# GpSimd's work on weight pieces in two halves, small VectorE operations one column at a time

## The reference

```python
q = (x @ Wq) ; k = (x @ Wk) ; v = (x @ Wv)          # 32 heads, 8 kv heads repeated 4 times
probs = softmax(where(causal, q k^T * 128**-0.5, -inf))
x = layernorm(x + (probs @ v) @ Wo)
weights = sparsemax(x @ W_router^T + b_router)       # 8 experts
ffn = x @ W_base^T + b_base + sum_e weights_e * (x @ lora_A_e) @ lora_B_e
out = layernorm(x + ffn)
```

## Time and profile before

| | |
|---|---|
| median of three runs | 689.89 us |
| the profiled execution | 687.37 us |
| its span | 685.3 us |
| TensorE busy with matmuls | 662.2 us (97%) |
| VectorE busy | 543.8 us (79%), 1525 instructions |
| ScalarE busy | 412.8 us (60%) |
| GpSimd busy | 279.7 us (41%), 424 instructions |
| granted TensorE clock, mean | 0.998 |

### The profile page before, as it was taken

How to read it: one execution, slowest core, us unless ns; L and a number is a source line. 1 busy time by engine, 2 the same in 40 slices (tenths; PEclk the granted TensorE clock), 3 DMA queues, 4 the chain that set the end, 5 groups by cost and what they waited for, 6 DMA issues and landing times.

```text
span 685.3 us, 11442 instructions
## 1 busy us (share of the span) xinstructions
PE 662.2 (97%) x3606; PEld 354.1 (52%) x3606; DVE 543.8 (79%) x1525; ACT 412.8 (60%) x1072; POOL 279.7 (41%) x424
## 2 busy tenths in 40 slices
PE   6798999999999999999999999999999999999996
PEld 3364545455554555454555555454555545445675
DVE  4899889876897679767888779767878776899774
ACT  1677566667647765667556764667656764766232
POOL 1576972167105661258004751248014550161132
PEclk9999999999999999999999999999999999999999
DMA  9347347363924256343924366444724335544411
GB/s 291 118 133 167 62 104 181 60 95 61 231 55 93 48 133 159 74 78 87 224 49 77 62 157 121 78 78 95 183 47 77 61 64 108 115 101 75 80 47 61
DMA packets 200780, 71.81 MB, mean 105 GB/s; under 512 B 169744, under 2 KB 192784, under 8 KB 200720
## 3 DMA queue, kind: packets, MB, share of 16 engines
q1 hardware_dynamic: 199376, 70.04, 46.7%
q10 hardware_dynamic: 1344, 1.05, 0.6%
HBM read 27.02 MB, written 2.10 MB: 42 GB/s over the span
## 4 chain that ended last, share of the span: by engine, by line
PE 83%; DVE 7%; DMA 3%; POOL 3%; issue 2%; SPq 1%; ACT 1%; POOLq 0%; DVEq 0%; ACTq 0%
PE bank L1128 21%; PE bank L1079 19%; PE bank L1118 13%; PE bank L1103 11%; PE bank L1091 4%; PE bank L1059 3%; PE bank L1160 3%; DMA pT<-p 2%; PE bank L1072 2%; DVE pr L929 2%; PE bank L1062 2%; DVE p L947 1%; POOL raw L678 1%; SPq L627 1%; PE bank L1171 1%
## 5 line engine op out<-in xcount | busy, mean ns | idle before, releaser
L678 POOL TENSOR_SCALAR raw<-raw,scale_of 128x512 f32<-128x512 f32 x76 | 121.0, 1593 | 162.0 <-ACT wk L740 66.2
L781 ACT ACTIVATE pr<-pr,mx 128x96 f32<-128x96 f32 (+15 forms) x256 | 131.4, 514 | 85.9 <-DVE mx L929 85.9
L790 ACT ACTIVATE p<-pr,ri 128x32 f16<-128x32 f32 (+15 forms) x256 | 118.8, 512 | 78.3 <-DVE ri L939 56.7
L1079 PE MATMUL bank<-xT,wq 128*128 128x512 f16 x720 | 164.4, 379 | 0.2 <-DVE v L849 0.2
L947 DVE SCALAR_TENSOR_TENSOR p<-pr,ri,p 128x256 f16<-128x256 f32 (+15 forms) x256 | 135.2, 572 | 35.2 <-ACT p L790 34.8
L929 DVE CUSTOM_DVE_ANT_0 pr<-bank,mask,back_of 128x32 f32<-128x32 f32 (+15 forms) x256 | 124.6, 494 | 43.3 <-PE bank L1103 42.8
L1103 PE MATMUL bank<-kT,qT 128*128 128x32 f16 (+15 forms) x768 | 124.4, 279 | 5.0 <-DVE qT L843 3.7
L1118 PE MATMUL bank<-pT,v 128*128 128x512 f16 x480 | 123.3, 379 | 3.0 <-DMA pT<-p 2.9
L1079 PEld LDWEIGHTS bank<-xT,wq 128*128 128x128 f16 x720 | 70.3, 98 | 82.2 <-DVE v L849 0.6
L691 POOL MEMSET p<- 128x64 f16 (+2 forms) x192 | 34.3, 206 | 161.8 <-DMA pT<-p 161.8
L1103 PEld LDWEIGHTS bank<-kT,qT 128*128 128x128 f16 x768 | 67.1, 98 | 64.2 <-issue 5.3
(11 more groups left out here) (121 smaller groups left out, 738.8 us busy)
## 6 DMA issues: line engine op xcount, KB each, us to landing
raw<-in_wo SPq DMA_DIRECT2D x32, 256.0 KB, 3.7
raw<-in_wq SPq DMA_DIRECT2D x30, 256.0 KB, 3.9
raw<-in_wk SPq DMA_DIRECT2D x8, 256.0 KB, 3.1
raw<-in_wv SPq DMA_DIRECT2D x8, 256.0 KB, 5.2
y<-in_x SPq DMA_DIRECT2D x1, 2048.0 KB, 13.2
pT<-p SPq DMA_TRANSPOSE x128, 3.7
out<-y SPq DMA_DIRECT2D x8, 256.0 KB, 2.0
pT<-in_xT SPq DMA_DIRECT2D x6, 256.0 KB, 7.7
```

Source lines behind the costliest of these rows:

```text
L678: eng.tensor_scalar(raw_of(name, key), raw_of(name, key), scale[0], None, ALU.mult).then_inc(sems["scaled"], 1)
L781: eng.activation(pr[:, t % 2, h, 0:w], pr[:, t % 2, h, 0:w], ACT.Exp, bias=mx[:, k:k + 1], scale=-1.0, accum_out=rs[:, k:k + 1]).then_inc( ...
L790: eng.activation(halves_of_probs(t, h)[0], pr[:, t % 2, h, 0:group(t, h)[1]], ACT.Copy, scale=ri[:, 1, k:k + 1]).then_inc(sems["p_hi"], 1)
L1079: made = eng.matmul(out, wq[:, g % 2, w, h, c * 128:(c + 1) * 128], xT[:, x, c, b * 512:(b + 1) * 512], start=c == 0 and w + x == 0, stop= ...
```

## The change

Two things are changed. GpSimd's scaling and subtraction of each scaled piece are each issued as two instructions of 256 columns; the second of the two signals. The subtraction of the six pieces without a scale stays whole. And VectorE's operations on two columns (`bound`, `rowpower`, `scale_of`, `back_of` and the product of `inv`) are each issued once for each column; the last one signals. Nothing else moves, and no wait is added.

```diff
-                        eng.tensor_scalar(raw_of(name, key), raw_of(name, key), scale[0], None,
-                                          ALU.mult).then_inc(sems["scaled"], 1)
+                        for cols in (slice(0, 256), slice(256, 512)):
+                            made = eng.tensor_scalar(raw_of(name, key)[:, cols], raw_of(name, key)[:, cols], scale[0], None, ALU.mult)
+                        made.then_inc(sems["scaled"], 1)
                         pool.wait_ge(*done("scaled", name, *key))
-                    eng.tensor_tensor(out=lo, in0=raw_of(name, key), in1=hi if scale else hi.bitcast(f32),
-                                      op=ALU.subtract).then_inc(sems["lo_pool"], 1)
+                        for cols in (slice(0, 256), slice(256, 512)):
+                            made = eng.tensor_tensor(out=lo[:, cols], in0=raw_of(name, key)[:, cols], in1=hi[:, cols], op=ALU.subtract)
+                        made.then_inc(sems["lo_pool"], 1)
+                    else:
+                        eng.tensor_tensor(out=lo, in0=raw_of(name, key), in1=hi.bitcast(f32), op=ALU.subtract).then_inc(sems["lo_pool"], 1)
...
-                    eng.tensor_scalar(bound[:, c0:c1], rowmax[:, c0:c1], 2.0 ** -40, None, ALU.max).then_inc(sems["bound"], 1)
+                    for c in range(c0, c1):
+                        made = eng.tensor_scalar(bound[:, c:c + 1], rowmax[:, c:c + 1], 2.0 ** -40, None, ALU.max)
+                    made.then_inc(sems["bound"], 1)
...
-                        eng.tensor_scalar(out, x, p[one], p[two], ALU.mult, ALU.mult).then_inc(sems["backs"], 1)
+                        for c in range(1 if stage in ("B", "C") else B):
+                            made = eng.tensor_scalar(out[:, c:c + 1], x[:, c:c + 1], p[one], p[two], ALU.mult, ALU.mult)
+                        made.then_inc(sems["backs"], 1)
...
-                    eng.tensor_scalar(ri[:, 1, k:k + 2], ri[:, 0, k:k + 2], TWO15, None, ALU.mult).then_inc(sems["ri"], 1)
+                    for c in (k, k + 1):
+                        made = eng.tensor_scalar(ri[:, 1, c:c + 1], ri[:, 0, c:c + 1], TWO15, None, ALU.mult)
+                    made.then_inc(sems["ri"], 1)
```

More of the change, by code:

```diff
@@ L875, in _ @@
                         dve.wait_ge(*done("most", *of))
-                    eng.tensor_scalar(bound[:, c0:c1], rowmax[:, c0:c1], 2.0 ** -40, None, ALU.max).then_inc(sems["bound"], 1)
+                    for c in range(c0, c1):
+                        made = eng.tensor_scalar(bound[:, c:c + 1], rowmax[:, c:c + 1], 2.0 ** -40, None, ALU.max)
+                    made.then_inc(sems["bound"], 1)
                     dve.wait_ge(*done("bound", stage))
-                    eng.tensor_scalar(rowpower[:, c0:c1].bitcast(i32), bound[:, c0:c1].bitcast(i32), 0x7f800000, None,
-                                      ALU.bitwise_and).then_inc(sems["rowpower"], 1)
+                    for c in range(c0, c1):
+                        made = eng.tensor_scalar(rowpower[:, c:c + 1].bitcast(i32), bound[:, c:c + 1].bitcast(i32), 0x7f800000, None,
+                                                 ALU.bitwise_and)
+                    made.then_inc(sems["rowpower"], 1)
                 elif name == "factor":
@@ L887, in _ @@
                     dve.wait_ge(*done("power", stage))
-                    eng.tensor_scalar(scale_of[:, c0:c1].bitcast(i32), power[:, c0:c1].bitcast(i32), -1.0, float(268 << 23),
-                                      ALU.mult, ALU.add).then_inc(sems["scales"], 1)
+                    for c in range(c0, c1):
+                        made = eng.tensor_scalar(scale_of[:, c:c + 1].bitcast(i32), power[:, c:c + 1].bitcast(i32), -1.0, float(268 << 23),
+                                                 ALU.mult, ALU.add)
+                    made.then_inc(sems["scales"], 1)
                     p = {of: power[:, c:c + 1] for of, c in COLUMN.items()}
```

## The result

The changed kernel takes 693.97 us (median of 10 runs, 692.57 to 696.59), the kernel before 688.65 us in the ten runs beside it (686.88 to 691.88). The ratio is 1.0081, with a 95% interval of 1.0069 to 1.0094: slower by 5.3 us, or 0.8%. (The 689.89 us from which the forecast set out was the median of three of these ten runs.) The profiled execution of the changed kernel has a span of 691.6 us, 6.3 us more than before.

A forecast was written before the change was run, and what follows sets the result against it. TensorE was taken to bound the long middle, VectorE only the pipeline's filling. Terms -1.7 - 0.3 + 1.5 + 1.4 + 0.5 = +1.4 us gave 688.8 us profiled, 691.3 us as median; range 686.8 to 695.5 us.

The forecast's parts named there:

- three signs of being wrong: Early waits don't move, a piece costs over 3.5 us, or the middle gains waits at steps that had none.
- the rival in which GpSimd falls behind: Each piece costs about 0.8 us more, half from VectorE getting in between: +6.7 us, 696.6 us; chance 0.18.
- Holding: GpSimd instructions hold up VectorE's two-column operations and L947; one-column `inv` products should take 0.15 to 0.17 us, none above 0.3.
- Added VectorE operations: 179 more one-column operations on VectorE, taken at 0.07 us each: 12.5 us of VectorE time, 8 to 28.
- The 0.5 us put down for `inv` at tight steps: Eight steps where a transpose waits for VectorE with TensorE close behind, 0.07 us each: 0.5 us (0 to 1.3).
- Price of a piece: GpSimd's added time per piece in halves: 0.35 us, at most 0.68; 28 us over 80 pieces (0 to 54).
- Early stretch: 38 to 63 us: VectorE less held up, gain 1.7 us (0 to 2.4); wait for Wv, gain 0.3 (-0.5 to 0.9).
- close to its own reader: In the Wv wait, the last of four x pieces in a row on GpSimd comes later, by some 0.35 us each.
- The steps with GpSimd on their path: Middle: one step in each of three repetitions, 1.5 us later (0 to 3); step at 544 us, 1.4 (0 to 2.7).
- corners that have about 1 us in hand: Within the +6.7 us rival: a few masked-corner clearings on GpSimd start to bind, +1 us.
- After 600 us: nothing: After 600 us the pieces have no scale and stay whole, so no change was expected there.
- The rival "doesn't do what it says": GpSimd's halves follow too closely to let VectorE in, L947 held as before: +2.6 us, 692.5 us; chance 0.13.

The follow-up runs named there:

- the columns alone: VectorE's two-column operations issued per column, GpSimd's pieces whole, against the kernel before: ratio 0.9979, and 0.9989 in a second set of runs.
- only the halves: GpSimd's scaling and subtraction in two instructions each, VectorE's operations on two columns as before, against the kernel before: ratio 1.0094.
- The kernel with quarters: The whole change with four GpSimd instructions of 128 columns in place of two of 256, against the kernel before: ratio 1.0693.
- the one with only group 1 in halves: The whole change, but only the eleven wk, wq, wv, wo pieces with group index 1 cut, the other 69 whole; against the kernel before: 1.0049.

## Why the prediction was right or wrong

The forecast was +1.4 us, so 691.3 us, with a range from 686.8 to 695.5 us; measured were +5.3 us and 693.97 us. The direction held, and 693.97 us lies in the range. The size didn't hold, and the range held in part by luck: the ten runs of the kernel before have a median of 688.65 us, not the 689.89 us of three from which the forecast set out, and its upper end, as a ratio to that, is 1.0081, just what was measured. Slower by over 0.5% had been given a chance of 0.20. Of its three signs of being wrong, two did not come (the early waits moved, a piece takes less than 3.5 us), and one did: the middle gained waits at steps that had none, at 79 and at 107 us. What the runs show is a mixture: a piece costs what the forecast took (the rival in which GpSimd falls behind, at +6.7 us, needed 0.6 us or more), while corners that had little in hand start to bind, which only that rival had, and had at 1 us.

- *Holding.* Right. One-column products are never held (155 ns at most), L947's longest fell by 0.4 us with no case more than 0.6 us over the fastest of its width, VectorE's busy time fell by 12 us.
- *Added VectorE operations.* 0.07 us apart, as taken: right. The 0.5 us put down for `inv` at tight steps doesn't show; the columns alone come out 0.1 to 0.2% faster. The Trainium skill's VectorE: DVE Perf Modes, section on the TRN2 errata, states a fixed cost of some 150 cycles at 0.96 GHz for each operation with its source on chip, by which 179 of them would be an estimated 28 us of VectorE time. The trace agrees for how long a single one lasts (median 150 ns), and not for what a second one behind it adds (0.07 us).
- *Price of a piece.* 0.40 us for the 0.35 taken, where nothing disturbs it. Right. With the halves that VectorE holds up, GpSimd is busy for 38 us more, 0.48 us a piece, where 28 us was the sum.
- *Early stretch.* Taken -1.7 and -0.3 us; measured in the waits -1.1 us (Q's split and `rowpower`) and +0.1 us (Wv, where the piece of x "close to its own reader" became what ends last). Little rests on the first of these: the same wait for Q's split near 63 us is 2.1 us in one profile of the columns alone and 0.2 us in the other.
- *The steps with GpSimd on their path.* This term was mis-sized, and it is the failure. I put down one step in each of three repetitions with 0.5 us each, and four pieces in a row at 544 us with 1.4 us. The latter wait went from 0.8 to 1.6 us. In the second and third repetition, from 250 to 430 us, the waits went from 0.7 to 3.7 us, where 1.0 us had been put for these two; the columns alone have 2.1 us there. What I left out is the longest row of pieces of all, 66 to 100 us: the page of the kernel before has no TensorE wait there, so I read that stretch as covered, and took GpSimd's average in the earlier trace rows, 216.04 of 530 us, for idle time everywhere. I never asked how long it works without a gap: from 70 to 103 us it is busy for 26.50 of 33 us. In that stretch ten pieces gain 0.40 us each, 4.0 us. GpSimd began it 1.0 us earlier (66.43 for 67.41 us) and no longer paused for 0.9 us, VectorE's getting in added some, and the corner of step 6 came 2.3 us later. The first transpose then held SyncE's queue for 2.41 us instead of 1.42, for a reason that was not looked for, and the second came 3.0 us later. TensorE waits for it 2.7 us, and before it 0.8 us for a piece of Wq at 79 us. The rival did name "corners that have about 1 us in hand", but priced them at 1 us in all.
- *After 600 us: nothing.* Wrong, by the columns and not by the halves: the two-column product was held by a whole subtraction of `wb` there, and 1.5 us of waits went.
- *The rival "doesn't do what it says"* falls: VectorE is let in between the halves, and GpSimd's second half then waits (0.89 us for 0.67).

The waits sum to +3.7 us of the 6.3 us of span. About 1.6 us more is TensorE's clock in this one execution (below), and some 0.5 us is there already at 28.41 us, where the kernel before starts its first scores at 27.93.

## What to carry to other kernels

An engine that is idle half of the time can still be the longest chain for 30 us. Before an instruction is cut in two, look for the longest stretch in which its engine works without a gap, multiply the added price by the pieces in it, and compare that with what the first waiter behind the stretch has in hand, not with the engine's busy share or with the waits that the bottleneck shows now. And where two engines hold each other up, change the short operation so that it isn't held (here one column in place of two, at 0.07 us each), not the long one so that it holds for less.

## What the runs showed of the hardware

- TensorE's clock fell in the wake of a wait, in one profile and not in its like. The changed kernel (from:to, length, busy of TensorE, weight loads, VectorE, ScalarE, GpSimd, granted clock):

```profile
104.00:107.70 3.70, 1.01 (x8) 0.45 (x7) 2.18 (x8) 2.21 (x6) 2.33 (x6) 0.96 0.82 194
107.70:111.00 3.30, 3.29 (x11) 1.28 (x12) 2.34 (x6) 2.02 (x6) 0.08 (x1) 0.52 1.05 303
```

  A mean of 0.52 is the lower of the two levels, 1.2 GHz, for nearly all of 3.3 us, about 1.6 us lost. TensorE had been busy for 1.01 of the 3.70 us before. With only the halves it waited 2.9 us at the same step, was busy for 1.49 of the 4.30 us before, and the clock stayed:

```profile
108.30:112.00 3.70, 3.66 (x22) 1.80 (x23) 2.31 (x6) 2.04 (x6) 0.10 (x1) 1.00 1.02 298
```

  The kernel with quarters, with waits up to 7.1 us, has a mean clock of 0.976 over its span, and the one with only group 1 in halves ran at 0.51 from 29.3 to 39.5 us, behind the first waits of the early stretch. What decides between the two was not settled.
- A GpSimd instruction that is added costs 0.26 us (scaling, 128 partitions, float32 in place) or 0.14 us (subtraction to float16), the same from one to two as from two to four.
- A GpSimd subtraction shuts out VectorE's product on 128x2, and not the reciprocal on 128x2 just before it, nor the product on 128x1. All 11 two-column products that start inside a subtraction are held, nine until 0.02 to 0.11 us after its end, two 0.36 and 0.46 us longer; nine reciprocals that start inside one take 151 to 167 ns, and 36 one-column products of the changed kernel at most 155 ns. The kernel before (VectorE, GpSimd):

```profile
96.66 0.17 DVE L937 RECIPROCAL ri<-rs 128x2 f32<-128x2 f32 x1
96.85 1.36 DVE L939 TENSOR_SCALAR ri<-ri 128x2 f32<-128x2 f32 x1
```

```profile
96.60 1.16 POOL L681 TENSOR_TENSOR wo_odd<-raw,wo_odd 128x512 f16<-128x512 f32 x1
```

- A GpSimd scaling shuts the same product out at its beginning and near its end only. In the kernel before, products that start in the first 0.47 us of an undisturbed scaling (1.57 us) end 0.70 to 0.72 us after its start, those that start 1.11 to 1.35 us after it end with the scaling, and those that start 0.8 to 1.0 us after it, or in its last 0.1 us, take 170 ns. One of the first kind (VectorE, GpSimd):

```profile
390.25 0.58 DVE L939 TENSOR_SCALAR ri<-ri 128x2 f32<-128x2 f32 x1
```

```profile
390.12 1.57 POOL L678 TENSOR_SCALAR raw<-raw,scale_of 128x512 f32<-128x512 f32 x1
```
